# Moving the experts' second bias from a GpSimd addition into a TensorE accumulation (vision tower with a mixture of experts, 1 core)

## What is computed

```python
logits = xf @ router_w
gate_vals, idx = top_k(logits, 2)
gates = softmax(gate_vals)
for e in range(8):
    h = relu(xf @ w1[e] + b1[e]) @ w2[e] + b2[e]
    y = layernorm(xf + h) * gamma[e] + beta[e]
    out = out + sum(where(idx == e, gates, 0)) * y
```

## Time and profile before

| | |
|---|---|
| median of 3 timed runs | 1307.33 us (1306.15 to 1309.15) |
| the profiled execution, its own time | 1298.23 us |
| its span in the profile | 1296.5 us |
| mean granted TensorE clock | 0.842 of full speed |
| TensorE busy | 941.3 us (73%) |
| VectorE busy | 820.5 us (63%) |
| ScalarE busy | 595.4 us (46%) |
| GpSimd busy | 449.3 us (35%) |

### The profile page before, as it was taken

One profiled execution on the slowest core, in us unless ns is written; L12 is line 12 of the kernel. 1 busy time (PEld: TensorE's weight loads), 2 busy tenths in 40 slices (PEclk: granted clock), 3 DMA queues, 4 the chain that ended last, 5 costly groups with the idle time before them and its releaser, 6 DMA issues.

```text
span 1296.5 us, 28777 instructions
## 1 busy us (share of the span) xinstructions
PE 941.3 (73%) x7760; PEld 762.1 (59%) x7761; DVE 820.5 (63%) x3204; ACT 595.4 (46%) x1544; POOL 449.3 (35%) x498
## 2 busy tenths in 40 slices
PE   2588788788767676686677676553999999999920
PEld 1488787655444454453455454432888888888810
DVE  2588878356545455454455454442889999899966
ACT  0221210277545455464466455431666666666610
POOL 3000000002331332322313322342677777777740
PEclk9988889797787787777878886855999999999965
DMA  6453320500110100100101100115422222222239
GB/s 122 84 73 57 56 31 1 157 32 23 34 32 18 33 28 21 33 24 25 33 16 33 33 28 21 33 42 147 154 65 71 73 72 70 66 73 73 73 129 395
DMA packets 69290, 83.73 MB, mean 65 GB/s; under 512 B 12307, under 2 KB 53958, under 8 KB 69114
## 3 DMA queue, kind: packets, MB, share of 16 engines
q1 hardware_dynamic: 54378, 55.08, 17.2%
q0 software_dynamic: 12416, 22.50, 5.5%
q10 hardware_dynamic: 2448, 5.57, 1.1%
HBM read 48.30 MB, written 35.71 MB: 65 GB/s over the span
## 4 chain that ended last, share of the span: by engine, by line
PE 33%; DVE 16%; issue 16%; another core or an unknown queue 13%; ACT 8%; POOL 5%; DMA 4%; POOLq 2%; SPq 2%; ACTq 1%; DVEq 1%
PE ps L651 6%; PE ps L882 4%; DVE arena L983 4%; PE ps L703 4%; POOL y_tokens L580 3%; PE ps L775 3%; DMA arena<-y_tokens 3%; PE ps L738 2%; ACT arena L1400 2%; PE ps L873 2%; PE ps L780 2%; DVE arena L1094 2%; PE ps L871 2%; PE ps L872 2%
## 5 line engine op out<-in xcount | busy, mean ns | idle before, releaser
L552 POOL DMA_INDIRECT x_slots<-arena x192 | 184.2, 959 | 456.0 <-ACT arena L1423 305.1
L580 POOL DMA_INDIRECT y_tokens<-arena x184 | 185.8, 1010 | 48.7 <-issue 43.1
L1544 ACT ACTIVATE arena<-ps,b_t 128x256 f32<-128x256 f32 x368 | 156.8, 478 | 87.4 <-PE ps L873 79.4
L882 PE MATMUL ps<-arena 128*128 x1472 | 181.8, 277 | 0.3 <-issue 0.3
L882 PEld LDWEIGHTS ps<-arena 128*128 128x128 f32 x1472 | 172.3, 192 | 2.4 <-issue 0.5
L1109 DVE TENSOR_TENSOR arena<-ps,arena 128x340 f32<-128x340 f32 x32 | 16.4, 512 | 204.7 <-ACT arena L1476 194.4
L703 PE MATMUL ps<-arena,wproj 128*128 128x340 f32 x256 | 131.4, 655 | 12.3 <-ACT arena L1438 5.0
L775 PE MATMUL ps<-arena,cst 128*128 128x340 f32 x64 | 45.7, 816 | 129.1 <-ACT arena L1476 124.4
L651 PE MATMUL ps<-wt,arena 128*128 128x128 f32 x960 | 132.6, 301 | 7.2 <-DVE h L1005 7.2
L651 PEld LDWEIGHTS ps<-wt,arena 128*128 128x128 f32 x960 | 127.1, 215 | 9.0 <-DVE arena L983 5.0
L1405 ACT ACTIVATE arena<-ps 128x340 f32<-128x340 f32 (+3 forms) x224 | 96.9, 459 | 43.3 <-PE ps L788 32.9
(11 more groups left out here) (202 smaller groups left out, 1954.9 us busy)
## 6 DMA issues: line engine op xcount, KB each, us to landing
arena<-x_slots SPq DMA_DIRECT2D x92, 130.0 KB
arena<-y_tokens SPq DMA_DIRECT2D x17, 640.0 KB, 14.6
h<-h_rows SPq DMA_DIRECT2D x1, 5440.0 KB
out<-h ACTq DMA_DIRECT2D x17, 320.0 KB, 9.0
arena<-x_in SPq DMA_DIRECT2D x64, 84.5 KB
arena<-x_in SPq DMA_DIRECT2D x64, 78.0 KB
h_rows<-h SPq DMA_DIRECT2D x32, 128.0 KB
x_slots<-arena POOLq DMA_INDIRECT x192
```

What stands on the lines that cost most here:

```text
L552: pool.indirect_dma_start(xs_dram, bass.IndirectOffsetOnAxis(ap=slot_i[par][0:rows, t, k:k + 1], axis=0), row[par][0:rows, k, t, :], None) ...
L580: pool.indirect_dma_start(y_dram, bass.IndirectOffsetOnAxis(ap=y_id[n % 2][:, k:k + 1], axis=0), y_sl[n % 2][:, k, :], None, bounds_check= ...
L882: ins = pe.matmul(ps[6 + m][:, 128 * k:128 * k + 128], hid[m][:, c, 128 * k:128 * k + 128], w2_sb[:, bass.ds(e, 1), c, :].rearrange("p o n ...
L1544: act.activation(hid[m][:, c, :], ps[2 + 2 * m + c // 2][:, SLOT * (c % 2):SLOT * (c % 2) + SLOT], ACT.Relu, bias=b1_t[:, bass.ds(e * FC + ...
```

## The change

`b2` is loaded as one row of 1,024 numbers into each of 3 partitions instead of 128 copies. At the end of VectorE's iteration 7 of the pair stage, nine chained instructions split it into three bfloat16 parts, one for each of the three partitions of `b2_t`. In the experts' stage each half of `second_layer` begins with a matmul of a 3 x 128 block of ones with the expert's 3 x 128 block of parts, which puts `b2` into the accumulation. GpSimd's `with_bias` is gone, so that `sums` adds the rows themselves. The semaphores `xb_ready` and its waits are gone, and `b2_loaded` and `b2_ready` are new; the order of everything else is kept.

```diff
@@ buffers
-        b2_all, gam_all, bet_all = (A2.take(NEXP, E_DIM) for _ in range(3))
+        gam_all, bet_all = (A2.take(NEXP, E_DIM) for _ in range(2))
+        b2_rest = A2.take(NEXP * E_DIM)
...
+        b2_part = [A2.take(NEXP * E_DIM, dt=BF16) for _ in range(B2_PARTS)]
...
-        x_b2 = [A3.take(2, E_DIM) for _ in range(2)]
...
+        b2_t = sb("b2_t", [B2_PARTS, NEXP, E_DIM], BF16)
+        b2_ones = sb("b2_ones", [B2_PARTS, 128], BF16)
@@ SyncE
-            for dst, name in ((b2_all, "L0_ffn_b2"), (gam_all, "L0_ffn_gamma"), (bet_all, "L0_ffn_beta")):
+            for r in range(B2_PARTS):
+                sp.dma_start(b2_rest[r:r + 1, :], a["L0_ffn_b2"].rearrange("(o e) n -> o (e n)", o=1)).then_inc(S["b2_loaded"], 16)
+            for dst, name in ((gam_all, "L0_ffn_gamma"), (bet_all, "L0_ffn_beta")):
@@ GpSimd
-            pool.wait_ge(S["fw_loaded"], 16 * (NEXP + 3))
+            pool.wait_ge(S["fw_loaded"], 16 * (NEXP + 2))
...
-            def with_bias(i, n, u, e):
-
-                pool.wait_ge(x_sl_loaded[n], 16 * u + 16)
-                need(pool, S["t_ready"], i - 1)
-                apart(pool)
-                b2 = b2_all[:, bass.ds(e, 1), :].to_broadcast([128, 2, E_DIM])
-                pool.tensor_tensor(x_b2[n % 2], x_sl[n][:, :, 0:E_DIM], b2, ALU.add).then_inc(S["xb_ready"], 1)
...
             def tile_iteration(at):
-                at(1, with_bias)
                 at(5, scatter_y)
@@ TensorE
+            pe.wait_ge(S["b2_ready"], 1)
...
+                bias = b2_t[:, bass.ds(e, 1), :].rearrange("p o n -> p (o n)")
                 for k in range(2):
+                    pe.matmul(ps[6 + m][:, 128 * k:128 * k + 128], b2_ones[:, :], bias, start=True, stop=False)
                     for c in range(FC):
                         ins = pe.matmul(ps[6 + m][:, 128 * k:128 * k + 128], hid[m][:, c, 128 * k:128 * k + 128],
                                         w2_sb[:, bass.ds(e, 1), c, :].rearrange("p o n -> p (o n)"),
-                                        start=c == 0, stop=c == FC - 1)
+                                        start=False, stop=c == FC - 1)
@@ VectorE
+            def bias_parts(p, par, half):
+
+                if not isinstance(p, int) or p != NEXP // 2:
+                    return
+                rows = slice(0, B2_PARTS)
+                dve.wait_ge(S["b2_loaded"], 16 * B2_PARTS)
+                for k in range(B2_PARTS):
+                    ch.link(dve.tensor_copy(b2_part[k][rows], b2_rest[rows]))
+                    if k < B2_PARTS - 1:
+                        ch.link(dve.tensor_tensor(b2_rest[rows], b2_rest[rows], b2_part[k][rows], ALU.subtract))
+                b2_flat = b2_t[:, :, :].rearrange("p e n -> p (e n)")
+                ch.link(dve.memset(b2_ones[:, :], 1.0))
+                ch.link(dve.tensor_scalar(b2_flat, b2_part[0][rows], ident[rows, 0:1], None, ALU.mult))
+                for k in range(1, B2_PARTS):
+                    ins = dve.scalar_tensor_tensor(b2_flat, b2_part[k][rows], ident[rows, k:k + 1], b2_flat, ALU.mult, ALU.add)
+                    ch.link(ins)
+                dve.sem_inc(S["b2_ready"], 1)
...
                 at(3, lower_weights)
+                at(3, bias_parts)
...
-                dve.wait_ge(S["xb_ready"], i + 1)
                 need(dve, S["norm_ready"], i - 1)
-                dve.tensor_tensor(res[m], ps[6 + m][:, 0:SLOT].rearrange("p (k n) -> p k n", k=2), x_b2[m],
+                dve.tensor_tensor(res[m], ps[6 + m][:, 0:SLOT].rearrange("p (k n) -> p k n", k=2), x_sl[n][:, :, 0:E_DIM],
                                   ALU.add).then_inc(S["t_ready"], 1)
```

More of the change, by code:

```diff
@@ L50 @@
 W_SCALE = 256.0
+B2_PARTS = 3
 N_CONCAT = float(CH * NSHIFT * SIDE * SIDE)
@@ L311, in build @@
             "slots_ready rank_used lg_ready max_ready best_ready pos_ready gate_done row_copied sc0 sc1 "
-            "base_ready q_copied k_copied og_ready nb1_ready nb2_ready w1_loaded fw_loaded w1_upper w1_split "
+            "base_ready q_copied k_copied og_ready nb1_ready nb2_ready w1_loaded fw_loaded b2_loaded b2_ready w1_upper w1_split "
             "cnt_ready cnt_ps tab_f_ready tab_ps pad_first pad_ready tab_ready pad_gone pad_stored xs0 "
             "xs1 xs2 xs3 xs4 xs5 norm_ready scl_ready gate_ready bns3_ready xt_ps xhi_ready xlo_ready "
-            "h_ps h_ready w2_ps xb_ready t_ready rstd3_stats rstd3_ready y_ready yg0 yg1 yl0 yl1 yl2 yl3 "
+            "h_ps h_ready w2_ps t_ready rstd3_stats rstd3_ready y_ready yg0 yg1 yl0 yl1 yl2 yl3 "
             "yl4 yl5 yl6 yl7 sum_ready rstd0_done nb_done xmn_done xhn_done tr_full tr_free y_full "
@@ L841, in _ @@
             pe.wait_ge(S["w1_split"], NEXP)
-            pe.wait_ge(S["fw_loaded"], 16 * (NEXP + 3))
+            pe.wait_ge(S["b2_ready"], 1)
+            pe.wait_ge(S["fw_loaded"], 16 * (NEXP + 2))
             copies = []
@@ L1259, in _ @@
             dve.wait_ge(S["pad_gone"], 16 * NEXP)
-            dve.wait_ge(S["fw_loaded"], 16 * (NEXP + 3))
+            dve.wait_ge(S["fw_loaded"], 16 * (NEXP + 2))
             def lower_half(i, n, u, e):
```

## The result

**Slower by 3.6%.** The changed kernel takes 1355.61 us (1352.6 to 1357.11) beside 1307.99 us for the kernel before, run on the same chip: a ratio of 1.0363, 95% interval 1.034 to 1.0385. The forecast was 1300.5 us, 0.5% faster, and its range of 1288 to 1310 does not hold the result.

A forecast was written before the change was run, and what follows sets the result against it. A two-tile loop through GpSimd's scatters and late TensorE signals was taken to bound the expert stage. Expert stage -9.8 and split +3 gave -6.8 us, taking 1307.33 to 1300.5 us; range 1288 to 1310.

The forecast's parts named there:

- I take 0.11 for one, 0.22 for the two: TensorE, expert stage: each bias matmul adds 0.11 us, two a tile 0.22, making the period 3.54 us.
- Rival 5: Expert stage: each bias matmul opens a hole in TensorE's float32 stream; at 0.27 us each, about 1329 us; chance 0.08.
- The loop stops binding: Expert stage: without GpSimd's addition the two-tile loop falls to 6.60 us, 3.30 a tile, below TensorE's floor of 3.32.
- It placed the second scatter behind the first relu and called the rest spare: Expert stage: relu stays prompt; the second layer's signal comes late, sums wait some 0.2 us, which VectorE can spare.
- The arithmetic (7.25 / 2 against 3.668): Expert stage before: loop from sums through scatters and relu sums to 7.25 us for two tiles, nearly the measured 3.668 each.
- Rival 4: Expert stage: late signals still hit the hidden layer, or the loop is not the cause; 3.67 a tile, about 1310; chance 0.10.
- The split: VectorE, pair stage iteration 7: splitting b2 takes about 9 us, mostly absorbed; 3 us lost, bounds 0 and 9.
- rival 3: Pair stage: the split of b2 costs its full 9 us, about 1306.5 us, no change; chance 0.10.
- VectorE was freed as forecast: Expert stage: the two sums take 0.60 us instead of 0.97, so VectorE's work falls from 3.39 to 3.02 a tile.
- an estimate of 3.48 us a tile: Expert stage: period at the skill's 81 ns a matmul, net gain some 5 us larger; set aside for the rows' slots.

The follow-up runs named there:

- k128: The changed kernel with the bias matmul over all 128 partitions, 125 of them zero; ratio 1.0272 to the kernel before.
- k65: The changed kernel with the bias matmul over 65 partitions, 62 of them zero; ratio 1.032 to the kernel before, one execution.
- matmul_only: The kernel before, GpSimd's addition kept, with the two 3-row bias matmuls a tile added on zeros; ratio 1.0249.
- no_matmul: The changed kernel without the bias matmuls, the second bias missing from its result; ratio 1.0242 to the kernel before.
- wait: The changed kernel, 3-row bias matmuls kept, with GpSimd waiting for a later tile's sums before it scatters; ratio 1.0226 to the kernel before.
- k64: The changed kernel with the bias matmul over 64 partitions, 61 of them zero; ratio 1.020 to the kernel before, one execution.
- apart: The kernel before, with GpSimd's addition moved between the two scatters of a tile instead of ahead of both; ratio 0.9914.

## Why the prediction was wrong

**The term "I take 0.11 for one, 0.22 for the two" was mis-sized.** It measured 0.35 and 0.70. The failed step is the choice of rows to price it by: all matmuls of the earlier trace rows have 128 contraction rows (L725 loads 85 columns of them), and the bias matmul has 3. L738 and L780 of the same trace had the price, 0.162 and 0.213 a slot. Rival 5 had the place ("nothing in TensorE's list of this stage has only 3 rows") and the right sign, with a threshold of 0.17 us; but its price of 0.27, also the upper bound, was that of an unpipelined record, and left out that the two neighbours are slowed too. It was given 0.08. k128 and k65 show that type and place were costed well: with 65 or 128 rows the price is 0.11, and the first tiles with 128 take 3.53. matmul_only gives the effect on the time: +2.5%.

**"The loop stops binding" was wrong.** The signals are late near scatters, as read from the earlier trace rows; the six traces of the table bear that out. But the prediction followed one of the signals of a tile, the first relu's. It placed the second scatter behind the first relu and called the rest spare. no_matmul shows another one late: that of the transposes, for which L1283 and the next hidden layer wait in the end. Without bias matmuls nothing but TensorE's floor of 3.32 should have bound, and the tile took 3.99, still about 3.86 if all that the clock can have cost is taken off. The arithmetic (7.25 / 2 against 3.668) had agreed, yet that was no test of what a shorter loop would do: GpSimd's addition also kept two tiles' scatters apart. Rival 4 said this ("the scatters earlier but not out of its way"), with a tile that stays at 3.67; that it could be worse than 3.67 was not among the cases.

**The two losses overlap.** 2.5% and 2.4% alone make 3.6% together, since with a TensorE of 4.02 us the late signals cost nothing for 60 tiles. Only after a disturbance do they return. Both kernels have a pause between the program's 305th and 306th indirect DMA, 3.2 us from start to start, before and after:

```profile
1122.21 1.00 POOL L580 DMA_INDIRECT y_tokens<-arena  x1 [0.16 <-issue]
1125.43 0.99 POOL L580 DMA_INDIRECT y_tokens<-arena  x1 [2.22 <-DVE arena L1273]
```

```profile
1144.27 0.97 POOL L578 DMA_INDIRECT y_tokens<-arena  x1 [1.54 <-DVE arena L1336]
1147.50 0.97 POOL L578 DMA_INDIRECT y_tokens<-arena  x1 [2.27 <-DVE arena L1336]
1148.78 0.97 POOL L578 DMA_INDIRECT y_tokens<-arena  x1 [0.30 <-issue]
1150.05 0.97 POOL L578 DMA_INDIRECT y_tokens<-arena  x1 [0.30 <-issue]
```

After it the changed kernel runs three scatters in a row and from there on alternates 2.92 and 6.75; the kernel before has its addition (1126.42) in between and recovers. `wait` shows that restoring an order on GpSimd is enough. That the pause starts the alternation is read from the trace; no run took the pause away, and k64, whose pause is the same (1137.09 to 1140.33), fell back to 4.02 us after it. So the pause alone doesn't decide, and what does stays open.

**The split: 3 us forecast, about 0 measured.** On VectorE it lies between 361.6 and 369.6 us, 8.0 for the expected 9:

```profile
L1143 DVE TENSOR_TENSOR arena<-arena x2: 1214/1214/1214, 362.3 to 364.3; 3x1024 f32<-3x1024 f32 x2
```

(1.19 had been worked out for it.) Two iterations of the pair stage around it take 25.5 + 12.5 = 38.0 us, before 18.0 + 20.1 = 38.1. The rest of the pair stage varies by more than that from kernel to kernel: the expert stage's first tile starts at 893.0 to 901.8 us in the eleven kernels with the split, and at 897.7 to 900.6 in the five without. The split was absorbed, as the prediction argued, and rival 3 falls.

**VectorE was freed as forecast.** L1315 takes 0.60 us for its two, at 1100.06 and 1104.08, also beside a scatter. It was worth nothing, VectorE not being the bound.

**The issue gap and the load.** The Trainium skill (TensorE: Matmul & The Clock Gate, Back-to-back issue gap) gives about 81 ns for a 128-column matmul in a sustained stream, from which an estimate of 3.48 us a tile was worked out. In k128 a bias matmul among float32 ones adds 109 ns and the first tiles take 3.53 us, so this trace does not agree. On the load itself, the Trainium skill (TensorE: Matmul & The Clock Gate, LDWEIGHTS) says that its time goes by columns, and that one of 32 rows takes as long as one of 128. The trace nearly agrees: L880's load takes 0.09 us at 3 rows and 0.10 at 128. So the length of the load was not the cost; that the short one does not run beside its neighbours was.

## What to carry to other kernels

Price a new matmul by a row with the same number of contraction rows, and count the slots of both neighbours. Here a matmul of 3 or 64 rows between full ones cost 0.35 us and one of 65 or 128 rows 0.11, so padding a short operand with zero rows can pay where it stands in a dense stream. An operation off the critical path may hold others in their place: before removing one from GpSimd's queue, ask where its indirect DMAs will fall relative to TensorE's signals, for each signal of the tile. Moving one instruction in that queue (`apart`) beat both kernels with the same work; it shifted VectorE's load as well, so look at both.

## What the hardware showed that was not expected

- A matmul of 3 or 64 rows among 128-row ones: 0.35 us, with its neighbours' slots at 0.21 and 0.21; of 65 or 128 rows: 0.11. A float32 one of one row: 0.61.
- TensorE's recorded semaphore updates are late in over half of the cases within 1.5 us of the start of an indirect DMA on GpSimd (858 of 1,492), and in 3% otherwise (28 of 1,067). Updates without a record of their own fall there too, 590 against 2. Why one is late and its neighbour isn't stays open, and so does whether spaced scatters would be harmless if all of them were spaced.
- A pause ahead of the program's 306th indirect DMA, 3.2 us from start to start, in the kernel before, in the changed one and in those of the experiments (3.6 in apart). Its cause was not looked into.
- One code with two periods: after the pause the changed kernel ran at 4.76 instead of 4.02 us a tile to the end of the stage.
- A clock that adds to the loss: in no_matmul the granted clock fell from 1.0 to 0.5 eight times in the stage, mostly after TensorE had stood idle for about 2 us.
